# First feed-forward: whole-number gate and up weights, two rounded products with the parts of x

## The reference

```python
SCALE = 1.0 / 127.0
wg = w_gate.astype(x.dtype) * SCALE      # (384, 128) whole numbers
wu = w_up.astype(x.dtype) * SCALE        # (384, 128)
wd = w_down.astype(x.dtype) * SCALE      # (128, 384)
gate = jnp.einsum('bsd,hd->bsh', x, wg)
up = jnp.einsum('bsd,hd->bsh', x, wu)
h = jax.nn.silu(gate) * up
return jnp.einsum('bsh,dh->bsd', h, wd)
...
x = x + _L0_attn_ref(_layernorm(x, axis=-1), ...)
x = x + _L0_ffn_ref(_layernorm(x, axis=-1), L0_ffn_w_gate, L0_ffn_w_up, L0_ffn_w_down)
x = x + _L1_attn_ref(_layernorm(x, axis=-1), ...)
```

## Time and profile before

| | us |
|---|---|
| runs of the kernel | 1136.63, 1144.24, 1147.08 |
| their median | 1144.24 |
| the profiled execution | 1135.98 |
| its span | 1134.2 |
| mean granted TensorE clock in it | 0.888 |

### The profile page before, as it was taken

How to read it: one execution, slowest core, us unless ns; L and a number is a source line. 1 busy time by engine, 2 the same in 40 slices (tenths; PEclk the granted TensorE clock), 3 DMA queues, 4 the chain that set the end, 5 groups by cost and what they waited for, 6 DMA issues and landing times. The chain is left out here.

```text
span 1134.2 us, 18018 instructions
## 1 busy us (share of the span) xinstructions
PE 917.4 (81%) x6494; PEld 592.5 (52%) x6494; DVE 677.8 (60%) x1706; ACT 433.0 (38%) x876; POOL 550.0 (48%) x430
## 2 busy tenths in 40 slices
PE   4559999999989878267999899994699997299993
PEld 2113333333333446164566676663697667199883
DVE  6756667767660255979677479999302475643334
ACT  2334665566555422014111356665344211032221
POOL 4335977897788611152312158888300001146661
PEclk9658999999997988658799699998799998599997
DMA  5700111011000000001000000030200000166665
GB/s 169 222 1 2 29 30 30 2 29 30 3 1 23 1 21 8 9 6 56 2 1 2 1 10 20 19 128 0 75 1 1 1 10 29 55 191 214 211 206 143
DMA packets 37815, 56.40 MB, mean 50 GB/s; under 512 B 5643, under 2 KB 25091, under 8 KB 37607
## 3 DMA queue, kind: packets, MB, share of 16 engines
q1 hardware_dynamic: 35238, 50.21, 14.5%
q0 software_dynamic: 2496, 5.12, 1.6%
HBM read 44.17 MB, written 10.94 MB: 49 GB/s over the span
## 5 line engine op out<-in xcount | busy, mean ns | idle before, releaser
L671 DVE TENSOR_REDUCE arena<-ps 128x2 f32<-128x1024 f32 (+2 forms) x192 | 177.3, 955 | 86.9 <-PE ps L487 55.5
L420 POOL TENSOR_TENSOR arena<-arena 128x1024 f32<-128x1024 f32 (+3 forms) x105 | 201.3, 1957 | 38.8 <-ACT arena L606 38.8
L606 ACT ACTIVATE arena<-ps 128x512 f32<-128x512 f32 (+3 forms) x320 | 138.8, 489 | 91.4 <-PE ps L519 57.6
L117 POOL TENSOR_SCALAR vareps<-meanvar 128x4 f32<-128x4 f32 x32 | 7.8, 245 | 234.6 <-DVE meanvar L98 234.6
L511 PE MATMUL ps<-arena 51*128 51x512 bf16 (+3 forms) x384 | 91.4, 345 | 18.0 <-ACT arena L606 6.8
L152 PE MATMUL ps<-ident,xn 128*128 128x128 f32 x128 | 27.2, 365 | 69.2 <-DVE xn L106 25.4
L511 PEld LDWEIGHTS ps<-arena 51*128 51x128 bf16 x384 | 26.9, 94 | 106.9 <-ACT arena L606 59.7
L2058 PE MATMUL ps<-arena 128*128 128x128 f32 x624 | 78.1, 279 | 0.0
L1389 PEld LDWEIGHTS ps<-arena 128*128 128x128 f32 x512 | 60.8, 192 | 30.7 <-ACT arena L1443 20.3
L2058 PEld LDWEIGHTS ps<-arena 128*128 128x128 f32 x624 | 74.6, 196 | 0.0
L420 POOL TENSOR_TENSOR xnT<-xnT,arena 128x1024 f32<-128x1024 f32 (+1 forms) x28 | 52.8, 1907 | 42.1 <-ACT xnT L606 42.1
(11 more groups left out here) (319 smaller groups left out, 1985.7 us busy)
## 6 DMA issues: line engine op xcount, KB each, us to landing
arena<-in_L_ffn_w SPq DMA_DIRECT2D x39, 512.0 KB, 4.2
arena<-scratch SPq DMA_DIRECT2D x32, 192.0 KB, 3.9
scratch<-arena SPq DMA_DIRECT2D x12, 256.0 KB, 3.9
arena<-in_L_ffn_w SPq DMA_DIRECT2D x8, 257.0 KB, 2.7
arena<-in_L_ffn_w SPq DMA_DIRECT2D x8, 256.0 KB, 4.0
arena<-expert_rows SPq DMA_DIRECT2D x8, 256.0 KB, 4.8
scratch<-arena SPq DMA_DIRECT2D x4, 384.0 KB, 5.1
scratch<-arena SPq DMA_DIRECT2D x12, 128.0 KB, 4.2
```

The lines of the kernel that those rows point to most:

```text
L420: nc.gpsimd.tensor_tensor(e, e, weight[:, at:at + k].unsqueeze(1).broadcast_to([P, 2, k]), ALU.mult).then_inc(weighed, 1)
L606: nc.scalar.activation(probs(g)[:, 2 * p + e, 0:wd], m.ps[:, BANK[h, e], 0:wd], ACT.Exp, scale=SCALE).then_inc(exps, 1)
L671: nc.vector.tensor_reduce(out, scores, AX.X, ALU.max, negate=True).then_inc(max_set, 1)
```

## The change

`l0_ffn` asks for the split of x. ScalarE (`widen`) casts the gate and up weights, still whole numbers, into a rounded tile `w_up`, and the down weights times 1/127 squared into the fp32 tile `w_down`; VectorE's `dequantise` goes. Each gate or up product becomes two rounded matmuls that add up in the same bank, the weights by `x_high` and by `x_low`. The factor 1/127 of the gate moves into Silu's scale, that of up into `w_down`. The part after sets aside the space of the rounded tiles. ScalarE's casts of x and GpSimd's subtractions come in through `Norm`, whose code is unchanged.

```diff
 def l0_ffn(nc, m, A, sem, sb, norm):
     F = 384
     FT = F // P
     SCALE = 1.0 / 127.0
+    m.rounded.fresh()
+    x_high, x_low = norm.split_xnT()
+    w_up = m.rounded.take("l0f_w_up", [P, 2, F], F32R)
     wi = sb("l0f_wi", [P, 3, F], I32)
-    w = sb("l0f_w", [P, 3, F])
+    w_down = sb("l0f_w_down", [P, F])
...
-    def dequantise(dve):
-        dve.wait_ge(w_in, w_all)
-        nc.vector.tensor_scalar(w[:, :, :], wi[:, :, :], SCALE, None, ALU.mult).then_inc(w_scaled, 1)
+    def widen(act):
+        act.wait_ge(w_in, w_all)
+        nc.scalar.activation(w_up[:, :, :], wi[:, 0:2, :], ACT.Copy).then_inc(w_set, 1)
+        nc.scalar.activation(w_down[:, :], wi[:, 2, :], ACT.Copy, scale=SCALE * SCALE).then_inc(w_set, 1)
...
             norm.wait_xnT(pe, c)
+            cs = slice(c * CH, (c + 1) * CH)
...
                 for half in range(2):
-                    nc.tensor.matmul(m.ps[:, 2 * (s % 2) + half, :], w[:, half, f * P:(f + 1) * P], m.xnT[:, c * CH:(c + 1) * CH],
-                                     start=True, stop=True).then_inc(up_done, 1)
+                    out, lhsT = m.ps[:, 2 * (s % 2) + half, :], w_up[:, half, f * P:(f + 1) * P]
+                    nc.tensor.matmul(out, lhsT, x_high[:, cs], start=True, stop=False)
+                    nc.tensor.matmul(out, lhsT, x_low[:, cs], start=False, stop=True).then_inc(up_done, 1)
...
-                                          w[:, 2, f * P:(f + 1) * P], start=(f == 0 and j == 0), stop=(f == FT - 1), skip_group_check=True)
+                                          w_down[:, f * P:(f + 1) * P], start=(f == 0 and j == 0), stop=(f == FT - 1), skip_group_check=True)
...
-        pe.wait_ge(w_scaled, 1)
+        pe.wait_ge(w_set, 2)
...
-            nc.scalar.activation(sg[:, s % 2, :], m.ps[:, 2 * (s % 2), :], ACT.Silu).then_inc(sg_done, 1)
+            nc.scalar.activation(sg[:, s % 2, :], m.ps[:, 2 * (s % 2), :], ACT.Silu, scale=SCALE).then_inc(sg_done, 1)
...
-                before_norm={"vector": dequantise})
+                before_norm={"scalar": widen})
...
 def l1_attn(nc, m, A, sem, sb, norm):
     H, HD = 16, 8
     HB = NT // 2
     SCALE = HD ** -0.5
+    sb("rounded", [P, 2 * T + 2 * 384])
```

More of the change, by code:

```diff
@@ L736, in l0_ffn @@
     w_in, w_all = norm.loads(1)
-    w_scaled = sem("l0f_w_scaled")
+    w_set = sem("l0f_w_set")
     up_done = sem("l0f_up_done")
```

## The result

Over 20 runs each the changed kernel took 1139.01 us in the median (1132.24 to 1144.37) and the kernel before 1144.45 (1136.63 to 1148.09). The ratio is 0.9949 with a 95% interval of 0.9931 to 0.9966, 5.8 us less, within the one per cent.

The account below looks back on a forecast made before the run. The part was taken to be bound by TensorE, with VectorE close behind. Gains of 4.5 + 1.4 + 0.9 = 6.8 us off 1144.24 gave 1137.4 us (0.6%), range about 1127.5 to 1146.

Parts of the forecast that it names:

- The price of a product: Gate and up products on TensorE: two rounded matmuls take 0.458 us instead of 0.86 at full clock, weight loads hidden.
- rival (b): Weight loads don't hide beside rounded matmuls on TensorE: only 1.5 us saved, 1142.7; chance 0.07.
- The start: Up to the first gate product: transposes 3 us earlier, mostly spent on the split; gain 0.4 us.
- The first two chunks: Up to the first down products: these begin at 413.9 instead of 418.36, with 1.0 us of waiting; gain 4.5 us.
- The third chunk: From its predecessor's down products: 6.9 us instead of 8.27, TensorE waiting 1.1 before the third step; gain 1.4 us.
- The fourth: Fourth chunk: 7.5 us instead of 8.36, TensorE waiting 2.1 behind VectorE's addition; gain 0.9 us.
- From the last down products to the last addition: End of the part, third group of down products to last addition (434.99 to 440.80): nothing changes.
- my own sign of being wrong: Forecast wrong if the clock is low anywhere after 411, matmul spacing is 0.4, or a later part shows a new wait.
- Rival (c): Slower: TensorE's clock doesn't rise because it waits in each chunk; 8.3 us more, 1152.5; chance 0.06.
- The sum: Whole part: 4.5 + 1.4 + 0.9 = 6.8 us, of TensorE's 9.6 and the start's 0.4; 4.2 go into waits.
- Rival (a): VectorE and ScalarE don't hold TensorE up: the 4.2 us of waits vanish, 11.0 saved, 1133.2; chance 0.13.
- Rival (d): The 6.8 us are saved here and lost among later parts as DMA timing differs; 1144.2; chance 0.12.

Follow-up runs that it names:

- the cast alone: Kernel before with ScalarE instead of VectorE casting the weights, products fp32, x not split; twice: ratios 0.9981 and 0.9960, part 35.97 and 36.77 us.
- The later additions: Changed kernel with VectorE's addition of a chunk moved behind the first gate times up of the chunk two later; ratio 0.9924, part 32.15 us.
- the three edits: Changed kernel with high part first, VectorE's additions later, ScalarE's copies after a chunk's first Silu; twice: ratios 0.9926 and 0.9932, part 29.51 and 29.52 us.

## Why the prediction was right

The forecast was 6.8 us less, 1137.4; measured are 5.8 less by the ratio and 5.7, 5.7, 6.4 and 6.6 in four traces of the part. By its steps, from the first trace unless said otherwise:

- The price of a product, with its weight load hidden, held: 0.23 us from one rounded matmul to the next (430.50 to 430.73). With it rival (b) fell. This trace speaks against the Trainium skill's rule (TensorE: Matmul & The Clock Gate, section Part 3: Packing small matmuls) that such loads overlap a matmul only in other rows of the array: here the same weights are loaded twice in a row at full height (0.19 us each), and the spacing stays at 0.23.
- The start: forecast 0.4, measured 0.71. The subtraction took about 1.3 instead of 1.40, and GpSimd's last root was done sooner (1.04 instead of the 1.31 that it took beside VectorE's dequantising). That the split would give back most of the 3 us won by the cast was right, and the cast alone shows it: first product 1.65 after x, with the split 4.14.
- The first two chunks: forecast 4.5, measured 5.19, because the clock rose at 411.2 in this trace, 7.1 after x; I had put 8.6 (409.2 less 400.56, with bounds of 8.4 and 9.1), which the third and fourth trace have (9.0, 8.6). There the down products begin some 0.8 later. A rise carried over from one other trace couldn't be sharper: it moves by 2 us between traces of one kernel, so the bounds were too narrow, and where 8.6 was met it was luck. Of the 1.0 of waiting 0.78 came.
- The third chunk: forecast 1.4, measured 1.33, with the wait 0.79 instead of 1.1. The fourth: forecast 0.9, measured 0.78, with 1.87 instead of 2.1. Both by the mechanisms named: ScalarE's copy and cast, and VectorE's addition with what hangs on it. The later additions took the wait of the fourth chunk away and left that of the third; with the copies later too, the third chunk's went.
- From the last down products to the last addition: forecast "nothing changes". This is the step that failed. In two of four traces the clock fell after the wait and 1.6 us went there, and with it my own sign of being wrong came, the clock at the low level after 411. In these two the total of 5.7 is near the forecast because two errors cancel in part: 7.30 gained up to the last down products instead of 6.8, then 1.6 lost; the 6.4 and 6.6 of the other two come by the steps forecast. Rival (c) had waits that cost the clock, but as a clock that never rises and 8.3 us; I had dismissed it with a stretch of 0.78 idle of 2 us, and the wait is 1.87. The Trainium skill (same page, A second HAM failure mode) tells of streams that cycle through PSUM banks and lose the clock again and again: in these traces it fell once in this part in two of four, and not at all in the other two.
- The sum: 9.6 and 0.4 less 4.2 of waits are 5.8 and not 6.8, so the sentence under the sum doesn't account for it. The 6.8 stands on the positions in the trace of before, which also hold its own wait and gaps (TensorE begins at 433.17 where its products alone would let it begin at 432.75) and a later rise of the clock (9.1 against 8.6); the new kernel drops these too.

The range held, and the change is inside one per cent. Rival (a), no holding up by VectorE, is not what the change does; it is about what the part becomes with the other orders (10.7 against my 11.0), in part by chance, since there the start is shorter and the clock rises sooner too. Rival (d), a loss in later parts, didn't happen to the change (5.8 in the whole, 5.7 to 6.6 in the part), though single traces of other kernels lose up to 4.5 us on the way.

What stays open: what decides whether the clock falls after a wait of 1.87 us, beyond that it went with an early rise in five traces; why the rise moves between traces; and whether the 5 us of the three edits appear in the whole, for which far more runs would be needed.

## What to carry to other kernels

When a matmul stream is halved, look at once at what its waits were hiding: here 9.6 us came off TensorE and only 1.4 to 3.2 of them arrived beyond what the moved cast alone brings, because the split delays the start, the eviction through two engines, placed in program order behind additions and norms, was next, and the clock rose later. Moving a small instruction off the engine that was busy just before a part starts can be worth more than a faster product (here 3.5 to 4.3 us against 1.4 to 3.2). And a new wait of two microseconds on TensorE can cost its clock as well (here in three of five traces), so put the consumer that frees the bank ahead of work that nobody waits for yet.

## What the runs showed of the hardware beyond that

ScalarE reads int32 at about the pace of fp32: 384 columns in 0.51 us, 768 in 0.84 and 1,152 in 1.16 with the scale, against 512 fp32 columns in 0.63 (L168) and 1,024 in 1.02. The granted clock rose 7.1, 7.2, 8.6 and 9.0 us after x in four traces of one kernel, and fell after a wait of 1.87 us in two of them. A normalisation on VectorE beside GpSimd's subtraction took 3.02 us instead of 1.08 (DVE L106 at 406.87, beside POOL L125 at 406.80 for 2.49); here nobody waited for it.
